# Attention exchange: the transfers back issued right behind the swaps in SyncE's order, the transfer out issued by ScalarE in its own queue

## The reference

```python
q = x @ Wq + bq
kv = x @ Wkv + bkv
k, v = jnp.split(kv, [H * DQK], axis=-1)
q = _rope(...); k = _rope(...)              # 16 heads of 64
scores = jnp.einsum('bhqd,bhkd->bhqk', q, k) * (1.0 / np.sqrt(DQK))
scores = jnp.where(causal[None, None], scores, -jnp.inf)
probs = jax.nn.softmax(scores, axis=-1)
out = jnp.einsum('bhqk,bhkd->bqhd', probs, v)
return out.reshape(b, s, H * DV) @ Wo + bo
```

## Time and profile before

| | |
|---|---|
| median of three runs | 2518.95 us |
| the profiled execution's own time | 2524.26 us |
| its span | 2521.5 us |
| attention phase, about | 480 to 2070 us |
| PE busy | 2282.4 us (91%) |
| DVE, ACT, POOL busy | 1808.1, 1435.9, 1440.1 us |
| queue q1 (all of SyncE's transfers) | 558.14 MB, 75.2% of 16 engines' span |

### The profile page before, as it was taken

How to read it: one execution, slowest core, us unless ns; L and a number is a source line. 1 busy time by engine, 2 the same in 40 slices (tenths; PEclk the granted TensorE clock), 3 DMA queues, 4 the chain that set the end, 5 groups by cost and what they waited for, 6 DMA issues and landing times. The chain is left out here.

```text
span 2521.5 us, 55108 instructions
## 1 busy us (share of the span) xinstructions
PE 2282.4 (91%) x17624; PEld 1780.9 (71%) x17624; DVE 1808.1 (72%) x3128; ACT 1435.9 (57%) x3741; POOL 1440.1 (57%) x1268
## 2 busy tenths in 40 slices
PE   7987899789999999999989999999999969986998
PEld 5753577577777777877777878778778756752676
DVE  6752477578887888887778878788879856731576
ACT  2321344376776777777667767767767733321343
POOL 1100345477787787887777877877778821100442
PEclk9999999899999999999999999999999989998999
DMA  7369654478988888898788888888888956469443
GB/s 253 122 254 392 228 184 146 114 207 233 239 239 232 229 241 231 238 246 230 213 226 237 225 235 236 241 230 234 236 226 230 256 158 232 178 261 405 137 150 104
DMA packets 340247, 561.56 MB, mean 223 GB/s; under 512 B 63616, under 2 KB 274176, under 8 KB 338944
## 3 DMA queue, kind: packets, MB, share of 16 engines
q1 hardware_dynamic: 339968, 558.14, 75.2%
HBM read 329.42 MB, written 161.48 MB: 195 GB/s over the span
## 5 line engine op out<-in xcount | busy, mean ns | idle before, releaser
L1439 POOL TENSOR_TENSOR att_z_sb<-att_z_sb,att_cos 128x512 f32<-128x512 f32 x255 | 337.6, 1324 | 309.9 <-DMA att_zs<-att_z_sb 309.9
L1547 DVE STREAM_TRANSPOSE att_farT<-att_got 128x1792 f32<-128x1792 f32 x128 | 261.7, 2045 | 211.3 <-DMA att_got<-last_tiles_blocks 211.2
L1442 POOL TENSOR_TENSOR att_z_sb<-att_z_sb,att_zs 128x512 f32<-128x512 f32 x255 | 341.4, 1339 | 20.0
L1440 POOL TENSOR_TENSOR att_zs<-att_zs,att_sin 128x512 f32<-128x512 f32 x255 | 344.9, 1353 | 0.0
L1643 ACT ACTIVATE att_far<-att_ps_w,att_nmax 128x512 f32<-128x512 f32 x256 | 173.9, 685 | 112.2 <-DVE att_nmax L1535 101.1
L1824 PE MATMUL att_ps_p<-att_farT,att_v_sb 128*64 128x128 f32 x3584 | 222.0, 275 | 0.0
L1824 PEld LDWEIGHTS att_ps_p<-att_farT,att_v_sb 128*64 128x64 f32 x3584 | 204.7, 138 | 0.0
L1447 POOL TENSOR_TENSOR att_kT_lo<-att_z_sb,att_kT_hi 128x512 fp32r<-128x512 f32 x128 | 163.5, 1277 | 22.3 <-ACT att_kT_hi L1627 22.2
L1055 POOL TENSOR_TENSOR com_b_kblk<-sh_blkmask,sh_kT 128x128 f32<-128x128 f32 x64 | 32.3, 525 | 243.4 <-POOLq L500 195.9
L1535 DVE TENSOR_REDUCE att_nmax<-att_ps_x 128x2 f32<-128x768 f32 (+1 forms) x256 | 165.1, 686 | 4.4
L180 POOL TENSOR_SCALAR dis_b_veps<-dis_b_mv 128x4 f32<-128x4 f32 x31 | 13.3, 431 | 265.8 <-DVE dis_b_mv L174 265.8
(11 more groups left out here) (248 smaller groups left out, 7028.4 us busy)
## 6 DMA issues: line engine op xcount, KB each, us to landing
last_tiles_blocks<-att_far SPq DMA_DIRECT2D x128, 896.0 KB, 6.3
att_got<-last_tiles_blocks SPq DMA_DIRECT2D x512, 224.0 KB, 4.5
att_zs<-att_z_sb SPq DMA_DIRECT2D x512, 128.0 KB, 3.4
att_R<-inverse_sums SPq DMA_DIRECT2D x256, 128.0 KB, 5.9
ffn_w<-in_e_W SPq DMA_DIRECT2D x30, 1024.0 KB, 9.7
ffn_wg<-in_e_Wg SPq DMA_DIRECT2D x24, 1024.0 KB, 13.2
x_normalised_transposed<-dis_b_xnT SPq DMA_DIRECT2D x32, 512.0 KB, 2.9
ffn_w<-in_e_W SPq DMA_DIRECT2D x32, 512.0 KB, 15.8
```

The lines of the kernel that those rows point to most:

```text
L1439: nc.gpsimd.tensor_tensor(z[:, m, i, :], z[:, m, i, :], cos[:], ALU.mult)
L1440: nc.gpsimd.tensor_tensor(zs[:, m, i, :], zs[:, m, i, :], sin[:], ALU.mult).then_inc(sin_s[i].sem, 1)
L1442: nc.gpsimd.tensor_tensor(z[:, m, i, :], z[:, m, i, :], zs[:, m, i, :], ALU.add).then_inc(sum_s[i].sem, 1)
L1547: nc.vector.transpose(farT[:].rearrange("p a (t r) -> p t a r", r=QUAD), got[:]).then_inc(turn_s.sem, 1)
```

## The change

SyncE's slot becomes swap(p+2), get(p-1), rows(p-1), spread(p-1). ScalarE issues `put(p)` itself, behind its exponentials of block 2 and ahead of `high_part(p-2)`. The count of landed puts is kept in two semaphores by parity of the unit; the waits on it follow. Data, sizes and buffers stay as they are.

```diff
-    put_s, got_s, turn_s = c("put", 16 * NP), c("got", 64 * NP), c("turn", NP)
+    put_s = [c(f"put{i}", 8 * NP) for i in range(2)]
+    got_s, turn_s = c("got", 64 * NP), c("turn", NP)
...
-            def put(j, u):
-                need_held(sp, exp_s, j, 8 * u + 4)
-                need_held(sp, got_s, j, 64 * (u - 1))
-                sp.dma_start(last_dram[u % 2], far[:, u % 2].rearrange("p b h a c -> p (b h a c)")).then_inc(put_s.sem, 16)
-
             def get(j, u):
-                need_held(sp, put_s, j, 16 * (u + 1))
+                need_held(sp, put_s[u % 2], j, 16 * (u // 2 + 1))
                 need_held(sp, turn_s, j, u)
...
                 if t.has(p - 1):
+                    get(j, p - 1)
                     rows(j, p - 1)
-                    get(j, p - 1)
-                if t.has(p):
-                    put(j, p)
-                if t.has(p - 1):
                     spread(j, p - 1)
...
             def exps(j, p, qt):
                 if qt in FAR:
-                    need(act, put_s, j, 16 * (p - 1))
+                    need(act, put_s[p % 2], j, 16 * (p // 2))
...
+            def put(j, u):
+                need_held(act, exp_s, j, 8 * u + 4)
+                need_held(act, got_s, j, 64 * (u - 1))
+                act.dma_start(last_dram[u % 2], far[:, u % 2].rearrange("p b h a c -> p (b h a c)")).then_inc(put_s[u % 2].sem, 16)
...
                 if t.has(p):
                     exps(j, p, 2)
+                    put(j, p)
                 if t.has(p - 2):
                     high_part(j, p - 2)
```

## The result

The changed kernel takes 2725.98 us median (2718.84 to 2747.22), beside 2519.26 us for the kernel before: ratio 1.0839, 95% interval 1.0775 to 1.0904. It is 207 us slower where 40 us less were forecast, outside the range. All of it is in attention: from the first wide scores to the last the trace has 1550 us before and 1753 after. From 600 to 2000 us the kernel before sends 114 transfers out, the changed one 102, so a slot went from 12.28 to 13.7 us.

The account below looks back on a forecast made before the run. A closed ring (turn, mask, reciprocals, rows, transfer back; 11.39 us) was taken to bound the kernel, PE nearly. Early get with ScalarE's issue gave 11.6 us ordinary slots: 48 us less, 8 taken back for x, 2519 to 2479 us; range 2455 to 2505.

Parts of the forecast that it names:

- The ring over turn, mask, reciprocals, rows and get: Attention slot before: a closed chain of 11.39 us, exactly the distance of two VectorE turns, holding back PE and ScalarE.
- get ahead of rows: SyncE's queue: get free 2.76 us earlier, landing 9.4 us behind the wide scores, so the ring is cut.
- rows and spread behind get: SyncE's queue: `rows` lands with get at 9.4 to 9.7 us, SyncE free at about 11.9, next swaps due at 12.05.
- just covered: End of SyncE's slot: `spread` finishes at about 11.9 us, before the next swaps fall due at 12.05.
- GpSimd's 2.2 us a slot: GpSimd's waiting slack, 250.4 us in all, claimed to absorb late swaps before the keys are late.
- the slots with loads of x: Three slots of eight loading or storing x: cover goes by up to a microsecond; 0.5 us an item, 8 us taken back.
- put in its own queue: Transfer out off SyncE: frees 0.34 us and two waits there, lands before get asks for it; worth nothing by itself.
- get would be three quarters done when put starts: DMA queues: the argument against the two queues mixing, that little of get remains when the transfer out starts.
- The issue on ScalarE: ScalarE's way to the copy of v: `put` delays `high_part` by 0.7 us, bounds 0.35 and 2.0.
- C: Rival: queues mix, SyncE sits behind `rows`, its ring reaches 12.8 us; 64 us slower, 2583 us; chance 0.16.
- A: Rival: ScalarE's issue of `put` is nearly free, 0.35 us; 39 us more gained, 2440 us; chance 0.18.
- D: Rival: get waits for put(p-1) as long as for `rows`; no difference, 2511 to 2526 us; chance 0.16 shared with another rival.

Follow-up runs that it names:

- the best version: Changed kernel with `rows` issued by ScalarE, `put` on SyncE between get and spread, and the loads of x moved ahead of `spread`: 2450.63 us, ratio 0.9721.
- 1.0041: Changed kernel with SyncE's order as before (swap, rows, get, spread) and `put` issued by ScalarE behind the copy of v: 2530.69 us.
- 0.9912: Changed kernel with `rows` issued by ScalarE behind its exponentials of block 3 and `put` on ScalarE behind the copy of v: 2499.76 us.
- the quartered transfer: Transfer out cut to its first quarter: changed kernel 2625.90 us, ratio 1.0412; changed kernel with `put` back on SyncE 2596.36 us, ratio 1.0286.
- 1.0135: Changed kernel with `rows` issued ahead of get on SyncE, `put` still on ScalarE ahead of the copy of v: 2557.99 us.
- 0.9992: Changed kernel with `rows` issued by ScalarE behind its exponentials of block 3, `put` still ahead of the copy of v: 2524.35 us.
- 1.0800: Changed kernel with ScalarE's issue of `put` moved behind `high_part` and the first copy of v: 2729.91 us.

## Why the prediction was wrong, point by point

**What bounded the kernel before: right in the main.** The ring over turn, mask, reciprocals, rows and get was there: with get early and `rows` elsewhere VectorE's wait fell from 186.0 to 98.4 and, in the best version, 58.9 us, and with the issue of `put` out of ScalarE's way as well the ordinary slots take 11.4 to 11.6 us, against 11.6 forecast. That it adds up to the distance of the two turns proved nothing by itself, since its parts are cut from that distance; the slot shown was longer, 12.50. The early get is worth 1.3 points (1.0041 to 0.9912). About two of the best version's 2.8 came with the loads of x, whose move wasn't tried in the kernel before.

**get ahead of rows: right about its issue, wrong about its landing.** In the changed kernel get is issued right behind the swaps. It should have landed by 9.4 behind the wide scores; in the slot shown that is 14.5, since the swaps are 3.4 us late and get itself needs 7.90 us.

**rows and spread behind get: this is the step that failed.** I had the parts: `rows` lands with get, SyncE stands until then, SyncE is free at about 11.9 and the next swaps are due at 12.05. From that 0.15 us of cover I concluded "just covered", and that lateness would be absorbed by GpSimd's 2.2 us a slot. Measured, `rows` lands 14.6 behind the wide scores on the mean, not 9.4 to 9.7, and the swaps go 3.2 behind them, not 0.43.

For an ordinary slot with one queue "just covered" was right: such slots took 11.76 us with `put` on SyncE. Two mistakes lie in the rest. First, get is now *behind* the swaps, so a late swap makes get late, which makes `rows` and `spread` late, which makes the next swap late: lateness enters the ring again, and an engine beside it doesn't absorb it. The mean issue of the swaps behind the wide scores in the changed kernel shows it go round. It is 0.5 us in the short slot 6, 1.9 in slot 7 (the short slot, 10.28 us, is shorter than the ring), 3.2 in slot 0 and 6.9 in slot 1 behind the loads, 4.4, 2.5, 2.7 and 3.4 in slots 2 to 5; only the long double slot, 16.8 us, makes up for it. Second, the slots with loads of x were priced at 0.5 us an item, 8 us in all. Behind the loads 6.8 us an item were lost, 4.7 with `put` on SyncE. SyncE's issues around one of these loads (the first line):

```profile
1254.31 0.47 SPq L1408 DMA_DIRECT2D sh_xt<-x_after_ffn  x1
1255.07 2.47 SPq L1370 DMA_DIRECT2D att_zs<-att_z_sb  x4
1257.87 1.78 SPq L1390 DMA_DIRECT2D att_got<-last_tiles_blocks  x4
1260.01 0.34 SPq L1375 DMA_DIRECT2D inverse_sums<-att_rsumT  x1
1270.58 1.30 SPq L1382 DMA_DIRECT2D att_R<-inverse_sums  x2
```

Here 512 KB more stand ahead of the swaps and of get, and SyncE stands 10.2 us before `spread`.

**put in its own queue: "worth nothing by itself" was a term of the wrong sign.** Measured against the same order with `put` on SyncE it costs 5.3 points in this ring, and in the versions with `rows` on ScalarE 0.2 points or less, within the intervals. In the slot shown get needs 1.5 us more to landing than before; `rows` needs 1.1 more than with `put` on SyncE (5.8 against 4.7, medians). I had written that get would be three quarters done when put starts. With the swaps late put goes 1.74 us behind get's first issue (1290.16) and meets most of its 7.90 us; from ScalarE's timeline of the slot shown above:

```profile
1291.90 0.33 ACTq L1643 DMA_DIRECT2D last_tiles_blocks<-att_far  x1
```

The rule of the Trainium skill (DMA: Bandwidth & Descriptors, section Queues, rings and completion order) that the DMA engines go round the queues with work agrees with the 100 us of the quartered transfer in the second queue against 5 us in the first.

**The issue on ScalarE: right in size, off in worth.** 0.7 us was taken, 0.68 stands in the trace. On the path it was worth 24 us (1.0135 to 1.0041) or 20 (0.9992 to 0.9912), where 0.7 us in seven slots of eight would be 78: the most likely reason is that where get is late, that wait covers it. In the changed kernel all of it is covered (1.0839 against 1.0800). No lock between the two issuers showed on ScalarE: its 128 issues of `put` took 0.33 to 0.37 us each.

**The rivals.** C, named with a chance of 0.16 and a price of 64 us, is what happened, at its place and by its mechanism. For ordinary slots its ring was right: 12.8 us forecast, 12.67 in the slot shown and 12.78 on the mean. Its price was short by a factor of three. It had mixing and loads in one 1.2 us for every slot and set the 12.8 against the mean slot of 12.28, where ordinary slots had taken 11.86; and each of the slots behind the loads lost 3.4 us, the double one 2.1. A's condition didn't come true (0.68 us stood, not 0.35), nor did D's (get went right behind the swaps).

## What to carry to other kernels

Before an issue is moved up in a queue, list what is issued behind it on the same engine and which of those the engine waits on: here 16 KB landed 4.6 to 6.2 us after issue (medians) behind a large transfer back, and 1.8 to 2.2 ahead of it. An in-order issuer that waits for such a landing hands the delay to everything behind. Then close the ring: follow the delayed issue until it comes back to the one that was moved; GpSimd's slack, outside the ring, didn't keep the lateness from going round, and a ring about as long as the slot hands a delay on until a longer slot takes it up. Price the irregular slots by themselves: with one queue the whole loss lay in them. The repair here was cheap: the 16 KB went to the other queue, the waiting engine got its data early, and the loads that nobody waits for soon went ahead of the stand.

## What the runs showed that I had not expected

The clock took part. The changed kernel's granted TensorE clock from 600 to 2000 us is 0.96 where it was 1.00, and 0.99 in the best version. Three stretches of one long slot of the changed kernel, columns as in the earlier trace rows, and PE's wait in the first of them:

```profile
1156.50:1161.50 5.00, 1.08 (x8) 0.71 (x9) 2.71 (x3) 1.10 (x2) 4.84 (x5) 0.84 0.20 40
1161.50:1165.00 3.50, 3.50 (x35) 3.34 (x32) 3.08 (x6) 1.95 (x5) 3.50 (x4) 0.50 0.84 230
1165.00:1172.00 7.00, 6.92 (x43) 5.89 (x39) 4.27 (x8) 4.90 (x16) 3.00 (x4) 0.87 1.07 247
```

```profile
1160.90 1.12 PE L1818 MATMUL att_ps_p<-sh_kT,att_v_sb 128*64 128x256 f32 x4 [3.92 <-ACT att_probT L1655]
```

PE had been busy 1.08 of 5 us, and the next 3.5 us run at 0.50, the lower level of 1.2 GHz. Over the 1400 us a matmul costs 1203.46/10405 = 115.7 ns of PE's busy time instead of 1311.75/11791 = 111.2; over the 13390 matmuls or so of attention (11791 x 1590/1400) this would be 59 us of the 207, an estimate from above. In the stretches shown the lower level comes behind the stall; how much of it is on the path wasn't tried.

No run left out the load of x or the short slot in the changed kernel. Its trace has the lateness begin behind the short slot (1.9 us in slot 7) and grow most behind the loads (6.9 in slot 1).
